# Two streams over four batch rows: attentions 0 and 1 side by side, then rests 2 and 3 side by side

## What is computed

```python
x = layernorm(x + L0_attn(x))   # "attention" of a batch row
x = layernorm(x + L0_ffn(x))    # "rest": 16 experts + a shared one, top 4
x = layernorm(x + L1_attn(x))   # "rest": a selective scan, 16 states x 256 channels
x = layernorm(x + L1_ffn(x))    # "rest": top-1 of 8 experts, with a capacity
```

## Time and profile before

| what | value |
|---|---|
| device time, median of 3 runs | 1391.71 us (1391.53 to 1392.82) |
| the profiled execution: span, first to last instruction | 1397.1 us |
| busy: PE, DVE, ACT, POOL | 899.8, 1001.4, 557.8, 84.1 us |
| share of the span: PE, DVE, ACT, POOL | 64%, 72%, 40%, 6% |
| mean granted PE clock, as a share of full speed | 0.774 |

### The profile page before, as it was taken

How to read it: one execution, slowest core, us unless ns; L and a number is a source line. 1 busy time by engine, 2 the same in 40 slices (tenths; PEclk the granted TensorE clock), 3 DMA queues, 4 the chain that set the end, 5 groups by cost and what they waited for, 6 DMA issues and landing times.

```text
span 1397.1 us, 29245 instructions
## 1 busy us (share of the span) xinstructions
PE 899.8 (64%) x11808; PEld 542.2 (39%) x11808; DVE 1001.4 (72%) x2303; ACT 557.8 (40%) x1250; POOL 84.1 (6%) x56
## 2 busy tenths in 40 slices
PE   4655757687656678687747567687747667471455
PEld 2534535454333245354424235354423335240122
DVE  5455553666689987665689987765779997654985
ACT  3232232465643332465553232366554232355310
POOL 0000000011000000011000000011000000030630
PEclk8556758788769779587758989698758879786896
DMA  4110110211223310121123210031033310112420
GB/s 144 32 39 10 33 40 11 64 39 38 68 65 85 77 31 11 39 70 39 40 73 94 76 42 6 14 92 39 10 93 91 80 50 4 43 34 62 118 63 8
DMA packets 85079, 72.20 MB, mean 52 GB/s; under 512 B 24784, under 2 KB 63696, under 8 KB 84752
## 3 DMA queue, kind: packets, MB, share of 16 engines
q1 hardware_dynamic: 84944, 70.34, 19.3%
HBM read 66.51 MB, written 3.80 MB: 50 GB/s over the span
## 4 chain that ended last, share of the span: by engine, by line
DVE 38%; PE 30%; ACT 13%; issue 13%; DMA 3%; SPq 2%; DVEq 0%; POOL 0%; ACTq 0%; POOLq 0%
PE bank L723 6%; DVE SG L1749 5%; PE bank L550 4%; PE bank L755 2%; DVE Y L1842 2%; ACT relu_s L1034 2%; PE bank L881 2%; DVE XP L1762 2%; DVE CV L1762 2%; SPq L486 2%; PE bank L831 2%; DVE ml L1477 2%; DVE bank L1749 1%; DVE big L1737 1%; PE bank L832 1%
## 5 line engine op out<-in xcount | busy, mean ns | idle before, releaser
L723 PE MATMUL bank<-onehot,tparts 128*32 128x256 bf16 x3840 | 137.0, 304 | 51.2 <-DVE onehot L1523 51.2
L723 PEld LDWEIGHTS bank<-onehot,tparts 128*32 128x32 bf16 x3840 | 110.7, 107 | 87.0 <-issue 75.0
L881 PE MATMUL bank<-XP,CO 128*128 128x512 f32 x128 | 84.2, 792 | 63.2 <-DVE XP L1760 34.4
L1749 DVE TENSOR_TENSOR_SCAN SG<-big 128x512 f32<-128x512 f32 x96 | 111.7, 1204 | 0.9
L1224 ACT ACTIVATE big<-DEL,Aneg 128x512 f32<-128x512 f32 x96 | 63.8, 714 | 102.7 <-DVE SG L1749 96.7
L1034 ACT ACTIVATE relu_s<-bank,nml 128x192 f32<-128x192 f32 (+1 forms) x128 | 52.8, 424 | 111.6 <-DVE nml L1482 111.6
L881 PE MATMUL bank<-CV,CO 128*128 128x512 f32 x128 | 74.3, 710 | 33.5 <-DVE CV L1762 21.2
L1477 DVE TENSOR_REDUCE ml<-bank 128x2 f32<-128x384 f32 (+1 forms) x64 | 33.7, 568 | 68.8 <-PE bank L658 37.6
L1523 DVE TENSOR_SCALAR onehot<-ib,CO 128x1024 bf16<-128x1024 f16 x160 | 69.9, 480 | 14.2 <-PE bank L723 12.8
L755 PE MATMUL bank<-GT,QBD 128*32 128x32 f32 x3072 | 57.2, 209 | 34.6 <-DVE G L1532 23.6
L550 PE MATMUL bank<-CO,relu_s 128*128 128x128 f32 (+2 forms) x256 | 46.6, 343 | 47.6 <-ACT relu_s L1034 47.6
(11 more groups left out here) (309 smaller groups left out, 1992.4 us busy)
## 6 DMA issues: line engine op xcount, KB each, us to landing
BC<-bc_rows SPq DMA_DIRECT2D x128, 256.0 KB, 4.4
ib<-idx_rows SPq DMA_DIRECT2D x64, 256.0 KB, 4.1
rows_bounce<-RO SPq DMA_DIRECT2D x256, 8.5 KB
big<-comb_rows SPq DMA_DIRECT2D x16, 256.0 KB, 4.5
big<-comb_rows SPq DMA_DIRECT2D x8, 512.0 KB, 8.5
W<-w SPq DMA_DIRECT2D x1, 2818.0 KB, 14.3
RB<-rows_bounce SPq DMA_DIRECT2D x16, 136.0 KB, 2.1
X<-x SPq DMA_DIRECT2D x4, 256.0 KB, 2.8
```

The lines of the kernel that those rows point to most:

```text
L723: m = mm(bank[2 + c % 2][32 * bb:32 * bb + 32, 256 * kind:256 * kind + 256], tparts[:, kt, part, 32 * kind:32 * kind + 32], onehot[:, n % ...
L881: mm(bank[5 + j][:, :], ident, hC[(n - 1) % 2][:, j, :], start=(n == 1), stop=(n == DS)).then_inc(ysum.sem, ysum.up())
L1749: m = dve.tensor_tensor_scan(state, decay, dBu[:, n % 2, j, :], 0.0, ALU.mult, ALU.add)
```

## The change

The five stages become two streams that never join. Each is a list of parts, and one phase of each is taken in turn; the second begins `LAG` = 7 phases, half a tile, behind the first:

```diff
-            weave(keys(0), iter(()))
-            weave(attention(0), iter(()))
-            close(0)
-            for b in range(1, B - 1):
-                weave(attention(b), rest(b - 1))
-                close(b)
-            weave(attention(B - 1, last=True), rest(B - 2))
-            close(B - 1)
-            weave(rest(B - 1, alone=True), iter(()))
+            def first():
+                yield from idle(begun)
+                yield from first_keys
+                yield from attention(0)
+                yield from attention(2)
+                yield from attention(3)
+                yield from rest(2)
+
+            def second():
+                yield from idle(LAG)
+                yield from keys(1)
+                yield from attention(1)
+                yield from rest(0)
+                yield from rest(1)
+                yield from rest(3)
+
+            for _ in both(first(), second()):
+                pass
```

Nearly all buffers exist twice. The second attention's and the second rest's share one piece of SBUF; one set each of QBD, the one-hot ring, GT and the weights stays for both. Four PSUM banks go to each stream:

```diff
+        attentions = (first_attention, second_attention, first_attention, first_attention)
+        rests = (first_rest, first_rest, second_rest, first_rest)
...
+            own.bank = bank[4 * n:4 * n + 4]
...
+            own.bank = bank[4 - 4 * n:8 - 4 * n]
```

An attention had five banks. With four, the local output lies in bank 2 of its own, ACT copies it out before the picks take that bank (a new copy for each tile), and the picks change the order of their two banks:

```diff
+                    act.wait_ge(ol_ps.sem, ol_ps.at(b, 2 * i + 2))
+                    A(own.On[:, 0, :, :].rearrange("p h c -> p (h c)"), own.bank[2][:, 256:512], ACT.Copy).then_inc(ol_sb.sem, ol_sb.up(b))
...
                         else:
-                            pe.wait_ge(pl_ok.sem, pl_ok.at(b, 2 * i + 2))
+                        elif c == 1:
+                            pe.wait_ge(ol_sb.sem, ol_sb.at(b, i + 1))
+                        elif i >= 1:
+                            pe.wait_ge(at_used.sem, at_used.at(b, i))
```

QBD is spread by ACT in all tiles of rows 0 and 1; before, DVE did the whole of row 0 and tiles 0 and 1 of the others:

```diff
-            return i < 2 or b == 0
+            return b >= 2 and i < 2
```

The expert steps turn through three banks in place of two, one step at a time under way as before in the paired rests; the `alone` way of writing the last rest is gone, so its drive is on DVE again, the gate's copy on ACT, and one expert step is under way at a time:

```diff
+        def gate_bank(k):
+            return (0, 1, 3)[2 * k % 3]
...
-                T, lag = turns(alone), 1 + alone
...
-                if not alone:
-                    drive(0)
+                drive(0)
```

More of the change, by code:

```diff
@@ L379, in build @@
[L379 to L397 removed]
+        x_copied = signal("x_copied")
@@ L399, in both, with idle @@
+        def idle(steps):
+            for _ in range(steps):
+                yield
         def both(first, second):
@@ L405, in both, with streams, attention @@
                 yield
-        def turns(alone):
-            return 3 if alone else 1
-        first_bank = (5, 0, 2)
-        def row_after(b):
-            return (b, 1)
-        def first_of(keys, begun):
-            return lambda b: begun if isinstance(b, int) and b == 0 else keys(b)
-        def spread_by_dve(b, i):
-            return i < 2 or b == 0
-        def rows_loop(keys, tiles, merges, close, rest):
-            def attention(b, last=False):
+        def streams(first_keys, keys, tiles, merges, rest, begun=0):
+            def attention(b):
                 tile_phases = tiles(b)
@@ L452, in _ @@
-        @block.sync
-        def _(sp):
+                yield from (both(row_end(), keys(following[b])) if b in following else row_end())
+            def first():
[12 more added lines that the diff above has]
+                yield from rest(3)
@@ L459, in keys, with tiles @@
                     yield
[L461 to L465 removed]
+            def tiles(b):
+                own = attentions[b]
                 for i in range(NT):
+                    if i == 2 and b in following:
+                        sp.wait_ge(x_copied.sem, x_copied.at(b, 1))
+                        sp.sem_inc(hold_sp, 1)
+                        load(following[b])
                     for _ in range(3):
@@ L495, in merges, with rest @@
                     yield
-            def rest(b, alone=False):
-                sp.wait_ge(rest_done.sem, rest_done.at(b, 0))
+            def rest(b):
+                own = rests[b]
+                sp.wait_ge(*space_free(b))
                 for _ in range(ROUTE_PHASES):
@@ L1286, in merges, with rest @@
                     yield
-            def close(b):
-                pass
-            def rest(b, alone=False):
-                pool.wait_ge(rest_done.sem, rest_done.at(b, 0))
+            def rest(b):
+                own = rests[b]
+                pool.wait_ge(*space_free(b))
                 for _ in range(ROUTE_PHASES + 2):
@@ new lines, in vector_program @@
+            dve.wait_ge(set_v.sem, set_v.now("setup"))
+            dve.transpose(rank_turn[:, :, :], first_attention.SR[:, 0:2, :]).then_inc(set_v.sem, set_v.up("setup"))
+            dve.wait_ge(set_v.sem, set_v.now("setup"))
+            assert set_v.rows["setup"] == SET_VEC
+            streams(keys(0), keys, tiles, merges, rest)
+        programs = (sync_program, tensor_program, scalar_program, gpsimd_program, vector_program)
+        for program in programs:
+            program(Count())
```

1656 lines of the change are left out of this document (835 added, 821 removed).

## The result

The changed kernel takes 1403.05 us (median of 4 runs, 1397.32 to 1405.05) against 1392.26 for the kernel before: a ratio of 1.0073, 95% interval 1.0048 to 1.0098. It is slower by a little; the forecast was 1358, with a range of 1308 to 1400.

The account below looks back on a forecast made before the run. No single engine was taken as the bound; uncovered stages and two chains' latency were. 59 + 293 + 626 + 48 + 299 + 40 = 1365, times 0.9961 = 1360, forecast 1358 us for possible bank gains; range 1308 to 1400.

Parts of the forecast that it names:

- the level of the attention pair: Attention 0 beside 1, steps 11 to 64: PE, DVE and ACT busy time over length, 1.85, giving 293 us.
- the slower rival: Attention pair: uncovered PBD and rotation waits make half tiles 48.1 us; half this effect taken, measured 1407; chance 0.13.
- the start: Steps 0 to 11: setup and attention 0 to its first picks 54 us, row 1's keys 5, together 59.
- full clock for a PE that two attentions keep busy: Attention pair, by the skill's clock rule: PE work near 161 us, pair 270 us in place of 293.
- The light lock: Attention pair: the attentions hold each other up a little, half tiles 39.4 and 41.8 us, measured 1379; chance 0.23.
- PBD behind the spread: Attention pair, tile's end: PE waits for PBD copies behind the other stream's QBD spread on ACT, 4.4 us a half tile.
- one-hot rows behind the rotation: Attention pair, DVE: one stream's one-hot rows wait behind the other's rotation, 3.1 us a half tile.
- the signs that the prediction gave for being wrong: Half tiles over 43 us, PE's or ACT's longest waits for the other stream, or middle losses exceeding what joins give back.
- The reason against it: Against slow attention pairs: half tiles would gain under 7 of 50 us, where attention beside rest gains a quarter.
- the joins: Ends of the middle stages: of 8.4 us with one stream or none, 6 us saved in each stage.
- The forecast of 626: Steps 64 to 184, attentions 2 and 3 beside rests 0 and 1: 313 us each, 626 together.
- steps 184 to 195: Rest 2's start beside rest 1's end: 42 and 47 us of work at level 1.85, 48 us.

Follow-up runs that it names:

- pbd_first: Changed kernel with the second stream's phase first only in steps where the first attention is in phase 6 and the second in 13; 1399.74 us, ratio 1.0055.
- onehots_ahead: Changed kernel with DVE making one-hot rows of a pick chunk one step earlier where the four-slot ring has room; 1385.44 us, ratio 0.9955 to the kernel before.
- before_ahead: The kernel before with one-hot rows made one step earlier where the ring has room; 1388.54 us, ratio 0.9976 to the kernel before.
- all_three: Changed kernel with one-hot rows a step ahead, DVE's QBD spread throughout attentions 0 and 1, and the second stream first where it picks; 1374.96 us, ratio 0.9895.
- the first experiments: Follow-up runs of edited kernels, compared with the kernel before; the text doesn't say which of them count as the first.

## Why the prediction was wrong

- **The term that failed is the level of the attention pair**, 1.85, which was chosen between the bounds 1.43 and 1.97. Work and clock were right (536 for 543, granted clock 0.80 for "near 0.8"). Measured is 1.66, the upper end of where the slower rival "would have to stay". 29 us of the miss are here, and 7 more at the start, where attention 1's keys and attention 0's last free phases already share the queues. The prediction read the Trainium skill (TensorE: Matmul & The Clock Gate, Part 1: The HAM clock gate) as full clock for a PE that two attentions keep busy, and 270 us by that; the pair was granted 0.80, with PE busy for 212.4 of 322.0 us.
- **What made the level low was named among the rivals, and priced too low.** The light lock had half tiles of 39.4 and 41.8 us; the slower rival put its turning point at 43.2. The mean of the six halves from 66.0 to 325.7 is 43.3, in pairs of about 48 and 38. The rival's two terms were PBD behind the spread and one-hot rows behind the rotation. The first is right in size (4.3 us the longest), but freeing PBD alone gave little (`pbd_first`). The second was too narrow: I counted the rotation's 3.1 us and left out that merge, top 8 and the maxima stand ahead of the one-hot rows as well, and that the maxima wait for PE, which waits for the one-hot rows. `onehots_ahead` takes 16.2 us off the pair, and with the spread and the order it is 23. Two of the signs that the prediction gave for being wrong are there: half tiles over 43 us, and a wait for PBD over 4.
- **The reason against it was wrong.** I took the gain of attention beside rest, a quarter, as what a pair of attentions would do. The earlier trace rows are levels of unlike chains; `before_ahead` shows that 16 us less of the same wait are worth 3 us there, in place of 18.
- **The middle stages:** the joins were to give back 12 us. They gave nothing: 643 us where the two like stages before took 635.1. The forecast of 626 was itself some 9 us too long for its own reasoning: it took the stage with keys twice (3 us), and rest 1's end (47 us of work) both here and in steps 184 to 195, while attention 1's last seven phases (36 us of work in attention 0, 221.5 to 251.5) stood nowhere: 11 us of work, an estimate of 6 us. This also is why the busy time of the stretch is 1180.3 us, and 1218.7 in the two stages that the prediction took: other phases lie in it, not less work in the same ones. By like stages the level fell from 1.89 (1197.3 / 635.1) to 1.84 (1180.3 / 643), and the time that is too much lies outside the scans. Restoring `TWICE`, the old alignment or another order gives nothing. What takes the place of the join isn't shown; the expectation that empty time at a seam is time saved when the seam goes was an assumption, and no run bears it out. The attention has one PSUM bank less and a new copy for each tile here too, which the prediction priced at nothing; no run takes them away.
- **The rests side by side did better than forecast:** 324.0 us for 347 up to rest 2's end. Until the first state the work was 253 us, not 266, and the level 252.8 / 129.5 = 1.95 in place of 1.85; DVE 189.8 of 194.5 us, 98%, in the scans in place of 95 and 90. The level of 1.6 that the slower rival had for the rests' first part did not come. That two rests 11 steps apart are less alike than two attentions is what I would say of the reason; no run tests it.
- **No lock in the shared rings,** as forecast: DVE waits for PE to free one-hot slots 8.2 us in all in the pair, 10 times.
- **The last 5 to 6 us** between the profiled execution and the median of the changed kernel's runs have no trace. The forecast came from a profiled span times 0.9961; for the changed kernel the factor is 1403.05 / 1395.5 = 1.0054. That alone is 13 of the 45 us between 1358 and 1403. It is spread between executions and no property of a kernel: the four executions of the changed kernel all take 1.8 us more than their span. With the same 1.8 the profiled one of the kernel before took 1399, 7 us above its median; that of the changed kernel is 6 us below its own (granted clock 0.774 and 0.783). So stages compared across these two traces flatter the changed kernel by up to one in a hundred.

Of the 36 us of the first 64 steps, the experiments account for 26 (attention 2's query matmul at 362.1 in `all_three`, at 388.1 in the changed kernel). Open are the 17 us of the middle stages, and 10 of the first 64 steps.

## What to carry to other kernels

When two streams share in-order queues, compare what each queue holds between a producer and its consumer, not only the sums: work made just in time stands behind the other stream's waits, and when both streams use the same two engines, a wait on one becomes a wait on the other and back. The pair of like work was the place for this here, and the level measured on unlike pairs didn't carry over to it. The cure is cheap, the same instructions issued one step earlier, as far as the buffers allow; try it before moving work to an idle engine, which may hold up the busy one, as POOL's products did with DVE's scans.

## What was unexpected of the hardware

- Beside a POOL product on SBUF data, two scans of 128x512 on DVE with both inputs in SBUF took 4.37 us in place of 2.34, and the POOL product 3.29 in place of 2.35. In the lone rest of the kernel before, where state and decay lay in PSUM and only the drive in SBUF, POOL's products of the same size ran beside the scans without any delay to either (2.35 us for the product and for the two scans), at 3.70 us a state. Which buffer an operand lies in decided whether a second engine helped or hurt.
- The edit that moves the QBD spread off ACT gave 10 us while it put 15.5 us of work on DVE, which was already the fuller of the two in the pair: 192.8 of 322 us leaves room, when the work falls into DVE's waits.
- The kernel before ran in 1391.53 to 1394.86 us in its first four runs, and in 1383.53 to 1403.24 over the 35 of the first experiments, half a per cent and more to either side. Differences of 5 us and less between two edits are left undecided above.
